# Layer 0's routing on VectorE spread over four slots of the attention instead of three, its counts and marks one slot later

## The reference

```
x = L0_attn_h
xn = layernorm(x)
x = x + L0_attn(xn) + L0_ffn(xn)      # causal softmax attention, 16 heads of 8; 8 experts, top 2
xn = layernorm(x)
x = x + L1_attn(xn) + L1_ffn(xn)      # retention, 8 heads of 16; 8 experts, top-p
```

```
router_logits = x_flat @ router_w.T + router_b
top_vals, top_ids = top_k(router_logits, 2)
top_probs = softmax(top_vals)
for e in range(8):
    tok, slot = nonzero(top_ids == e, size=256, fill_value=(N, 0))
    y = a * (b * sigmoid(b)) @ W_out[e]      # a, b: products of x_pad[tok] with W[e], V[e]
    out = out.at[tok].add(y * w)
```

## Time and profile before

| | |
|---|---|
| median of 3 runs | 770.96 us (769.45 to 771.61) |
| profiled execution, first to last instruction (span) | 765.3 us |
| TensorE matmul busy | 703.9 us, 92% |
| VectorE busy | 546.6 us, 71% |
| ScalarE busy | 419.5 us, 55% |
| GpSimd busy | 327.7 us, 43% |
| chain that ended last | TensorE 75%, VectorE 9%, issue 5%, ScalarE 4%, DMA 3%, GpSimd 2% |

### The profile page before, as it was taken

One profiled execution on the slowest core, in us unless ns is written; L12 is line 12 of the kernel. 1 busy time (PEld: TensorE's weight loads), 2 busy tenths in 40 slices (PEclk: granted clock), 3 DMA queues, 4 the chain that ended last, 5 costly groups with the idle time before them and its releaser, 6 DMA issues.

```text
span 765.3 us, 17690 instructions
## 1 busy us (share of the span) xinstructions
PE 703.9 (92%) x6133; PEld 526.3 (69%) x6133; DVE 546.6 (71%) x1053; ACT 419.5 (55%) x802; POOL 327.7 (43%) x433
## 2 busy tenths in 40 slices
PE   5787788998899978989898999999999999999997
PEld 4643445556755547757666888888888888888885
DVE  6878997885678866779886766666665666666665
ACT  5645665676477678677664444444444444444442
POOL 3765643783758860147694631212122221222222
PEclk9999999999999999999999999999999999999999
DMA  6984655431134420012114611112121212111100
GB/s 188 261 239 137 179 133 201 167 95 49 51 120 129 142 85 1 12 33 61 54 43 117 156 52 56 56 41 69 41 69 41 69 41 59 50 52 58 41 15 14
DMA packets 63795, 66.51 MB, mean 87 GB/s; under 512 B 6512, under 2 KB 41840, under 8 KB 63728
## 3 DMA queue, kind: packets, MB, share of 16 engines
q1 hardware_dynamic: 62128, 63.23, 27.7%
q0 software_dynamic: 1024, 2.12, 1.0%
q10 hardware_dynamic: 576, 0.27, 0.1%
HBM read 47.46 MB, written 17.99 MB: 86 GB/s over the span
## 4 chain that ended last, share of the span: by engine, by line
PE 75%; DVE 9%; issue 5%; ACT 4%; DMA 3%; POOL 2%; SPq 1%; ACTq 0%; POOLq 0%; DVEq 0%
PE ps L1763 25%; PE ps L1992 22%; PE ps L1876 3%; DVE m L1241 3%; PE ps L1683 3%; PE ps L1587 3%; PE ps L1796 2%; PE ps L1831 2%; PE ps L1593 2%; PE ps L1597 2%; PE ps L1897 1%; DMA qk_parts<-qk_p 1%; PE ps L1601 1%; PE ps L1688 1%; PE ps L1580 1%
## 5 line engine op out<-in xcount | busy, mean ns | idle before, releaser
L963 ACT ACTIVATE f_h<-ps 128x512 fp32r<-128x512 f32 x256 | 153.3, 599 | 197.6 <-PE ps L1763 197.6
L1463 DVE SCALAR_TENSOR_TENSOR f_l<-ps,f_h 128x512 fp32r<-128x512 f32 x256 | 175.9, 691 | 112.5 <-ACT f_h L963 111.3
L1763 PE MATMUL ps<-x_hl,w_h 128*128 (+1 forms) x512 | 200.3, 391 | 0.0
L783 POOL TENSOR_TENSOR acc<-acc,yt 128x512 f32<-128x512 f32 x55 | 70.9, 1289 | 249.8 <-DVE yt L1501 249.8
L877 ACT ACTIVATE probs<-ps 128x1536 f32<-128x1536 f32 x64 | 92.8, 1450 | 34.4 <-PE ps L1606 33.8
L1763 PEld LDWEIGHTS ps<-x_hl,w_h 128*128 128x128 f32 x512 | 96.1, 188 | 19.6
L682 POOL TENSOR_SCALAR_AFFINE_SELECT probs<-probs 128x512 f32<-128x512 f32 x128 | 78.4, 637 | 59.8 <-ACT probs L877 59.5
L1992 PE MATMUL ps<-f_l,w_h 128*128 128x512 f32 x256 | 99.8, 390 | 1.3 <-DVE f_l L1463 1.3
L1992 PE MATMUL ps<-f_h,w_h 128*128 128x512 f32 x256 | 99.7, 390 | 0.0
L1763 PE MATMUL ps<-x_hl,w_l 128*128 (+1 forms) x256 | 99.6, 389 | 0.0
L1992 PE MATMUL ps<-f_h,w_l 128*128 128x512 f32 x256 | 99.6, 389 | 0.0
(11 more groups left out here) (225 smaller groups left out, 1328.2 us busy)
## 6 DMA issues: line engine op xcount, KB each, us to landing
gate_b<-gate_rows SPq DMA_DIRECT2D x64, 256.0 KB, 3.3
qk_parts<-qk_p SPq DMA_DIRECT2D x16, 512.0 KB, 3.8
k_st<-qk_parts SPq DMA_DIRECT2D x64, 96.0 KB
q_st<-qk_parts SPq DMA_DIRECT2D x64, 96.0 KB
y_tok<-zero SPq DMA_DIRECT2D x8, 512.0 KB, 2.9
w_raw<-in_w_e SPq DMA_DIRECT2D x16, 256.0 KB, 2.7
x_rows<-xn_rows SPq DMA_DIRECT2D x8, 260.0 KB, 3.2
w_up<-in_w_up SPq DMA_DIRECT2D x8, 256.0 KB, 2.7
```

Source lines behind the costliest of these rows:

```text
L783: nc.gpsimd.tensor_tensor(acc[:, :], acc[:, :], yt[:, e % 2, :], ALU.add).then_inc(summed, 1)
L963: nc.scalar.activation(r32(f_h[:, m % 4, :]), ps[:, m % 4, :], ACT.Relu).then_inc(f_hi, 1)
L1463: nc.vector.scalar_tensor_tensor(out=r32(f_l[:, m % 4, :]), in0=ps[:, m % 4, :], scalar=0.0, in1=f_h[:, m % 4, :], op0=ALU.max, op1=ALU.su ...
L1763: last = nc.tensor.matmul(dst, r32(lhs[i]), r32(rhs[j]), start=(k == 0), stop=(k == 2))
```

## The change

Two constants go up by one, `weigh_best` and `mark_best` for the second choice move from slot 1 to slot 2, `pick_first` for the second choice from slot 2 to slot 3, `choose` from slot 3 to slot 4, and TensorE's `count` waits in addition for the first division, because bank 7 by then holds the turned output of group 0.

```
-COUNT = 4
-MARK = 9
+COUNT = 5
+MARK = 10
@@ gpsimd, slot(g)
-                if num(g) in (0, 1):
-                    weigh_best(num(g))
-                if num(g) == 3:
+                if num(g) in (0, 2):
+                    weigh_best(num(g) // 2)
+                if num(g) == COUNT - 1:
                     choose()
@@ vector, slot(g)
-                if n in (1, 2):
-                    pick_first(n - 1)
-                if n in (0, 1):
-                    mark_best(n)
+                if n in (1, 3):
+                    pick_first(n // 2)
+                if n in (0, 2):
+                    mark_best(n // 2)
@@ tensor, count()
                 pe.wait_ge(counted, 1)
+                pe.wait_ge(wv_put, COUNT - 4)
```

## The result

| | before | changed |
|---|---|---|
| median of 20 runs each | 770.94 us | 767.70 us |
| ratio, 95% interval | | 0.9956 (0.9944 to 0.9969) |
| profiled execution: span | 765.3 us | 763.8 us |
| its own time in the runs | unknown | 766.44 us |
| TensorE, VectorE, GpSimd busy | 703.9, 546.6, 327.7 us | 703.2, 545.6, 328.7 us |

The change is faster by 3.2 us (0.44%), where 1 us was forecast and the range began at 768.0. The direction and most of the mechanism held; the size did not. The lines that follow are from the profile of the changed kernel, timeline of VectorE, with the openings of slots 2 to 6 and 8 to 14 and the moved operations; they answer to the earlier trace rows.

What follows compares the result with a forecast made beforehand. It took VectorE's order of work to bound slots 1 to 20, at full TensorE clock. Gains of 0.05 and 0.98 us, 1.03 off the 765.3 us span, gave 764.3, plus 5.66 made 770.0 us; range 768.0 to 772.1.

Steps and rivals of the forecast that it cites:

- The term of slots 12 and 13: Slots 12 and 13: near ties between VectorE's marks and GpSimd, 6.60 us taken between 5.96 (won) and 7.61 (lost); 7.58 before.
- Part 1: Slots 1 to 3, second choice moved: 0.79 us gained in slot 1, mostly lost behind GpSimd's cut; 0.05 us taken, bounds 0.00 and 0.80.
- Part 2: Slot 4 and the counts, now in slot 5: the swap and the added wait of `count` cost zero.
- Part 3: Slots 8 to 20, index and marks meeting another pattern of work: 0.98 us saved, bounds -1.6 and +0.03, +0.6 if slot 8 is late.
- rival A: Slots 3, 12 and 13: L1137 keeps its turn (0.54 instead of 0.05), ties won (0.64 more); 768.8 us, chance 0.2.
- theory C: Follow-up theory, slot 2: shorter TensorE wait, shorter clock falls, giving the gain beyond the marks' 1.6 us; mean clock about 0.003 higher.

Runs made afterwards that it cites:

- e7: The change plus six extra matmuls, results unused, keeping TensorE busy at the start of slot 2; 768.17 us, ratio 0.9954 to the kernel before.
- e1: The change run again with no edit, beside the kernel before; 767.90 us, ratio 0.9973.
- e5: The change plus a small unused VectorE reduction ahead of the marks of slots 12 and 13; 769.61 us, ratio 0.9983 to the kernel before.
- e3: The kernel before with only counts and marks one slot later, second choice left in slots 1 and 2; 768.36 us, ratio 0.9976.
- e4: The kernel before plus nine extra matmuls, results unused, keeping TensorE busy in slot 2; 770.50 us, ratio 1.0009.
- e8: The change plus six extra matmuls in slot 2 and the second choice's subtraction moved to slot 4; 767.49 us, ratio 0.9958 to the kernel before.
- e9: The kernel before profiled again without edit, on another chip; 785.73 us, with 783.51 for before beside it.

## Why the prediction missed

Two steps failed. The term of slots 12 and 13 was mis-sized by 0.6 us. And the forecast priced the whole change by the order of work at full clock, with nothing for a fall of the clock; in the runs the change was worth 1.2 to 1.6 us more than that order explains. The first step is shown. For the second, the runs show that falls occur, and leave open how much of the rest is theirs.

**Part 1 was right.** The moved `mark_best(1)` is covered in slot 2, TensorE's wait fell to 1.77 us (forecast 1.8), the cut holds L1134 and then L1137, and of the 0.79 us gained in slot 1 almost nothing is left when slot 4 opens: 64.94 - 54.86 = 10.08 us after slot 1 in e7, 10.17 before. Where the clock falls in slots 2 and 3, L1134 gets ahead of the cut (0.42 us in the first profile and in e1), and then TensorE is what slot 4 waits for.

**Part 2 was right.** Slots 4 to 7 took 2.77, 4.07, 2.77 and 3.05 us in e7 (forecast 2.77, 4.13, 2.77, 3.05). The added wait never showed: in the first profile the count waited 0.24 us, for `choose`, which the disturbed clock had made late, and in e7 it did not wait.

**Part 3 had one term mis-sized.** It said "I take the middle, 6.60" for slots 12 and 13; they took 6.02 or 6.03, both ties won, in all seven profiles that have these marks undelayed, and lost only when e5 delayed them. The 0.09 us by which VectorE was due ahead were enough, as the 0.12 us of the earlier trace rows had been; the middle was a hedge between two outcomes of which the nearest row favoured one. The others: slot 8 4.07 (forecast 4.01), slot 10 4.05 (4.05), slot 11 3.02 (2.98), slot 20 3.43 (3.44). With 6.02 the sum would have been 1.61 us in place of 1.03; measured at full clock 1.62. So half of rival A came true, the ties, and its other half, L1137 keeping its turn, did not. That the sum agrees to 0.01 us is in part luck: slot 5 was 0.06 us shorter and slot 8 0.06 us longer than forecast. But the corrected sum gives 769.4 us, still inside the range and still 1.7 us above what was measured.

On slot 8, where the Trainium skill (GPSIMD Engine Reference, Key points) said that a one-input instruction in a two-port mode contends as well, L1159 took 0.39 us in the first changed profile against the 0.34 us of before, ending 0.05 us after the cut beside it. The trace agrees with the rule in kind; the price was 0.05 us and not the 0.13 that the prediction had estimated without its working. In the trace of before L1159 began together with a copy of GpSimd's, both at 78.04, so its 0.34 us were probably no undisturbed time.

**What was missing.** The prediction said of the stretch that it ran "at full TensorE clock" and worked with this one execution. Most executions are not like it: the 35 spans of before in the set of e1 have a median of 768.2 us, and only one is as short as 765.3 (765.2). The difference of 5.66 us was taken for what lies around the span; in the later runs that part is 2.5 us, and the rest was this execution's good fortune. This did not move the forecast, which subtracts the gain from the same 770.96; it hid that a usual execution has losses that this profile does not show. The wait of 2.57 us in slot 2 was priced only by what comes after it in VectorE's order. It is also a place where the clock can fall, and the shorter wait of 1.77 us is another.

How much of the miss is the clock's can be estimated from the runs. Over the 70 runs of before and the 32 of the change that have span and clock on record, the mean spans lie 2.95 us apart, and a straight line through both puts 0.4 us on each 0.001 of mean granted clock. The change's mean of 0.9921 lies 0.0017 above the 0.9904 of before: 0.7 us. At equal clock 2.3 us are left (95% interval 1.8 to 2.7), of which the order of work in slots 1 to 20 explains 1.62. The 0.7 us are those of falls anywhere in the kernel, and the runs lie in part on different chips.

**What stays open.** Why the change has the higher mean clock, and whether the falls in slots 2 to 5 have to do with it: the mean of a whole run (0.9911 and 0.9898 for two sets of before, 0.9926 and 0.9913 for the change) has falls from all stages in it, a profile shows one execution, and e1, e3 and e4 each went against what theory C wanted. Nor is it known where the 0.7 us lie that remain at equal clock. The later stages do not show them: from slot 21 to slot 63 the profiles on the chips of e1 to e8 take 146.4 to 147.7 us, 146.55 in the first of before and 146.65 in the first of the change, and from the first cast of layer 1's weights to the end the two kernels differ by no more than 0.5 us; what lies between took 135.3 us before, and 134.5 and 136.2 in the first two profiles of the change. That the clock has a part in the medians is argued, not shown.

## What to carry to other kernels

Where two engines' instructions shut each other out, read the time from the start of the one to the end of the other in the profile, and forecast the new order by who arrives first; 0.1 us of arrival was worth 0.5 to 1 us. Moving work by a slot pays or costs mostly by the company it meets there, not by the load that it takes off. And before a forecast is anchored to one profile, see how its span and its granted clock stand to the runs; a wait of TensorE can go on costing after it has ended, 2.0 us behind that of slot 2 in e9.

## What the runs showed of the hardware

- The VectorE instructions with two SBUF inputs and the GpSimd instructions looked at here shut each other out, and the later one waits for the whole of the other: a mark took 0.68 us ahead of half a cut and 1.57 behind a GpSimd mark of 1.05 that began 0.02 us sooner (e5). 32 columns took 0.62 us behind half a cut and 0.18 without, even right behind another VectorE instruction of the same kind.
- A fall of TensorE's clock can turn a near tie between two other engines: it delayed the cut by more than VectorE's work, so that L1134 took 0.42 instead of 0.84 us. The slot was longer all the same (3.71 us in e1, 3.48 in e7).
- The same wait of 2.57 us was followed by full clock in one execution and by half clock in another (e9); a wait of 1.77 us was followed by half clock too.
- Six to nine matmuls whose results nobody uses, put into a wait at 59 us, came with 1.2 to 1.8 us more of waiting for a weight load at 415 us, and with 1.3 to 3.3 us more from 405 us to the end.
